# The gated one-hot of the last block: built with slots on the partitions from positions and scores spread through DRAM, instead of turned on TensorE

## The reference

```python
capacity = max(1, int(Sz * 2.0 / E) + 1)                       # 33 of 128 tokens
scores = softmax(einsum('bsd,ed->bse', x, router_w), axis=-1)  # E = 8
gate_vals, sel_idx = top_k(swapaxes(scores, 1, 2), capacity)   # for each sample and expert
tokens = x[b_idx, sel_idx]
h = gelu(einsum('becd,edh->bech', tokens, w1) + b1)
y = einsum('bech,ehd->becd', h, w2) + b2
out = zeros_like(x).at[b_idx, sel_idx].add(y * gate_vals[..., None])
```

## Time and profile before

| | us |
|---|---|
| three runs | 1085.27, 1085.51, 1091.91 |
| median | 1085.51 |
| span of the profiled execution, first to last instruction | 1077.5 |
| TensorE busy in it | 966.2 |
| DVE, ACT, POOL busy | 642.9, 571.7, 468.3 |

### The profile page before, as it was taken

One profiled execution on the slowest core, in us unless ns is written; L12 is line 12 of the kernel. 1 busy time (PEld: TensorE's weight loads), 2 busy tenths in 40 slices (PEclk: granted clock), 3 DMA queues, 4 the chain that ended last, 5 costly groups with the idle time before them and its releaser, 6 DMA issues. The chain is left out here.

```text
span 1077.5 us, 23011 instructions
## 1 busy us (share of the span) xinstructions
PE 966.2 (90%) x8722; PEld 747.5 (69%) x8726; DVE 642.9 (60%) x2007; ACT 571.7 (53%) x1209; POOL 468.3 (43%) x752
## 2 busy tenths in 40 slices
PE   4889998998999799988989999888888999999998
PEld 2556666565656566777877887766667777778787
DVE  3657777677778564665763333446888457466241
ACT  4768887777676465423334332123333845755553
POOL 6246675758686744665520000233445244213010
PEclk9989999999999899999999999989999999999999
DMA  7756443323332120000002331300000331521421
GB/s 179 188 137 163 114 122 80 85 72 105 84 99 70 41 84 7 15 12 6 6 26 67 108 108 54 111 20 15 20 21 11 92 100 25 94 80 40 138 65 53
DMA packets 72942, 78.56 MB, mean 73 GB/s; under 512 B 8469, under 2 KB 64132, under 8 KB 72832
## 3 DMA queue, kind: packets, MB, share of 16 engines
q1 hardware_dynamic: 67104, 69.61, 23.2%
q0 software_dynamic: 4096, 6.84, 3.0%
q10 hardware_dynamic: 1632, 0.64, 0.3%
HBM read 38.25 MB, written 11.68 MB: 46 GB/s over the span
## 5 line engine op out<-in xcount | busy, mean ns | idle before, releaser
L1286 DVE TENSOR_REDUCE arena<-pb 128x8 f32<-128x1024 f32 (+1 forms) x128 | 128.4, 1007 | 60.0 <-PE pb L647 56.5
L1780 ACT ACTIVATE arena<-pb 128x1024 f32<-128x1024 f32 (+1 forms) x128 | 130.8, 1022 | 58.9 <-PE pb L663 51.0
L2292 POOL DMA_INDIRECT arena<-yd,arena x64 | 63.9, 999 | 141.4 <-issue 141.3
L1834 ACT ACTIVATE arena<-pb 128x256 f32<-128x256 f32 x128 | 48.0, 383 | 131.0 <-PE pb L832 103.6
L831 PE MATMUL pb<-XLT,arena 128*128 128x256 f32 x256 | 80.2, 396 | 10.0 <-DVE arena L1445 7.5
L680 PE MATMUL pb<-arena 77*32 77x128 f32 (+1 forms) x2048 | 85.1, 285 | 0.0
L2171 POOL DMA_INDIRECT xd<-XB,arena x64 | 64.0, 1000 | 33.1 <-issue 19.2
L832 PE MATMUL pb<-XLT,arena 128*128 128x256 f32 x256 | 78.0, 387 | 0.0
L2030 ACT ACTIVATE arena<-pb,arena 128x264 f32<-128x264 f32 x128 | 54.7, 482 | 37.4 <-PE pb L1135 37.3
L2088 POOL TENSOR_SCALAR arena<-arena 128x4 f32<-128x4 f32 x48 | 9.4, 196 | 147.2 <-DVE arena L1241 144.8
L1441 DVE SCALAR_TENSOR_TENSOR arena<-arena,pb 128x256 f32<-128x256 f32 x128 | 53.0, 414 | 25.5 <-ACT arena L1834 19.7
(11 more groups left out here) (233 smaller groups left out, 2386.1 us busy)
## 6 DMA issues: line engine op xcount, KB each, us to landing
arena<-arena SPq DMA_DIRECT2D x190, 128.0 KB, 2.4
arena<-in_pe SPq DMA_DIRECT2D x32, 514.5 KB, 3.7
arena<-in_pr SPq DMA_DIRECT2D x8, 768.0 KB, 5.0
arena<-arena SPq DMA_DIRECT2D x43, 77.0 KB, 2.2
xd<-arena SPq DMA_DIRECT2D x8, 320.0 KB, 3.0
arena<-xd SPq DMA_DIRECT2D x8, 320.0 KB, 5.7
yd<-arena SPq DMA_DIRECT2D x8, 320.0 KB, 5.2
XO<-in_x SPq DMA_DIRECT2D x8, 256.0 KB, 3.2
```

The source lines that it names most:

```text
L1286: e.tensor_reduce(NM[i % 2][0][:, b, 4 * h:4 * h + 4, :].rearrange("p t h -> p h t"), sc, AX, ALU.max, negate=True).then_inc(v_max, 1)
L1780: e.activation(PT[n % 2][0:nk, :], bk2[1][0:nk, :], ACT.Exp, scale=SC8).then_inc(a_exp, 1)
L2292: e.indirect_dma_start(G[x % 8], None, yd, bass.IndirectOffsetOnAxis(ap=IDG.bitcast(U32)[:, k, b:b + 1], axis=0), bounds_check=None, oob_i ...
```

## The change

OTP is written with slots on the partitions at once. Slots are cut in three groups of 11 per expert (SLW = 11), so that a group has 8 x 11 = 88 partitions (RT). SP writes CS and TK of a unit to DRAM (`keep_places`), and at step 9 reads them back (`spread_places`), expert by expert, broadcast over the 11 partitions of the expert, to REP (88 x 8 samples x 2 x 128). At steps 33 to 40 DVE computes `ot`: for each of the three groups the position row is compared with the slot number of the partition (a new constant) and multiplied by the score row, in one instruction. OTP has three buffers now, so `ot` of a sample waits for `place` of the third sample before it. `og`, `gated` and `ot` on ScalarE are gone. `yt` writes YT in the order sample, group, expert, slot; `back` and `place` use three groups of 88 instead of 99, 99 and 66; `ys` is one activation instead of two.

```diff
@@ SP
+            def keep_places(u):
+                L.wait_ge(v_cs, u + 1)
+                L.wait_ge(v_tk, 2 * u + 1)
+                e.dma_start(pd[u, :, 0, :], CS[u % 2]).then_inc(d_pd, 16)
+                e.dma_start(pd[u, :, 1, :], TK[u % 2]).then_inc(d_pd, 16)
+
+            def spread_places(u):
+                L.wait_ge(d_pd, 32 * (u + 1))
+                if u:
+                    L.wait_ge(v_ot, 8 * u)
+                else:
+                    L.wait_ge(p_dn, 16)
+                for x in range(8):
+                    src = pd[u, :, :, :].rearrange("(b e) n t -> e b n t", e=8)[x].unsqueeze(0)
+                    e.dma_start(REP[SLW * x:SLW * x + SLW], src.to_broadcast([SLW, 8, 2, 128])).then_inc(d_rp, 16)
+
             for t in range(SLOT0, SLOTS + 1):
+                for g in group_at(t, 34, 1):
+                    keep_places(g // 2)
                 for u, k in esteps(t):
+                    if k == 9:
+                        spread_places(u)
                     if k in range(18, 34, 2):
@@ TensorE
-            def gated(u, b):
-                x = 8 * u + b
-                B = 2 + b % 2
-                og = OHP[b % 4][1].rearrange("p e s -> p (e s)")
-                L.wait_ge(g_og, x + 1)
-                L.wait_ge(*free[B])
-                for k, (a, n) in enumerate(TI):
-                    ins = e.transpose(bat(bk[B], k)[0:n, :], og[:, a:a + n], ident)
-                ins.then_inc(p_ot, 1)
-                free[B] = (a_ot, x + 1)
@@ place
-                L.wait_ge(a_ot, x + 1)
+                L.wait_ge(v_ot, x + 1)
@@ VectorE
+            def ot(u, b):
+                x = 8 * u + b
+                L.wait_ge(d_rp, 128 * (u + 1))
+                if x >= 3:
+                    L.wait_ge(p_bo, x - 2)
+                for k in range(3):
+                    ins = e.scalar_tensor_tensor(OTP[x % 3][:, k, :], REP[:, b, 0, :], CST[0:RT, C_SL + k:C_SL + k + 1],
+                                                 REP[:, b, 1, :], ALU.is_equal, ALU.mult)
+                ins.then_inc(v_ot, 1)
+
             def yt(u, k):
...
-                e.tensor_scalar(YT[:, :, k * CAP2:(k + 1) * CAP2], bk[4][:, 0:N8].rearrange("p (b s) -> p b s", b=8),
+                to = YT.rearrange("p b (k e s) -> p b k e s", k=3, e=8)[:, :, :, k, :]
+                e.tensor_scalar(to, bk[4][:, 0:N8].rearrange("p (b k s) -> p b k s", b=8, k=3),
                                 EWP[q % 4][:, 1028:1029], None, ALU.add).then_inc(v_yt, 1)
...
                         yt(u, (k - 16) // 2)
+                    if k in range(33, 41):
+                        ot(u, k - 33)
                     if k == 39:
                         put(2 * u)
@@ ScalarE: ot is removed, and ys becomes
-                e.activation(o[:, 0:2, :].rearrange("p k t -> p (k t)"), bk[B][0:99, 0:256], ACT.Copy)
-                e.activation(o[0:66, 2, :], bk[B][0:66, 256:384], ACT.Copy).then_inc(a_ys, 1)
+                e.activation(flat(YSP[x % 3]), bk[b % 3][0:RT, 0:384], ACT.Copy).then_inc(a_ys, 1)
@@ POOL
-            def og(u, b):
-                x = 8 * u + b
-                o, g_ = OHP[b % 4]
-                L.wait_ge(v_oh, x + 1)
-                if x >= 4:
-                    L.wait_ge(p_ot, x - 3)
-                e.tensor_tensor(g_, o, SCO[u][:, b, :].unsqueeze(2).to_broadcast([128, 8, CAP2]), ALU.mult) \
-                    .then_inc(g_og, 1)
```

More of the change, by code:

```diff
@@ L364, in program @@
         TK, WK, M8, CS = ([r(64, n) for _ in range(2)] for n in (128, 128, 8, 128))
-        OHP = [(r(128, 8, CAP2), r(128, 8, CAP2)) for _ in range(2)]
+        OHP = [r(128, 8, CAP2) for _ in range(4)]
         rl = Region(KEEP, SF0)
@@ L376, in program @@
         EWP.append(r(128, 1029))
-        OHP += [(r(128, 8, CAP2), r(128, 8, CAP2))]
         ro = Region(SET0[3], SH0)
-        OHP += [(r(128, 8, CAP2), ro(128, 8, CAP2))]
         OUTP = [Region(ZB0, SET0[0])(128, GB, 128), ro(128, GB, 128)]
-        YSP = [r(99, 3, 128)]
         r = Region(SH0, WORDS)
-        OTP = [r(99, 3, 128) for _ in range(9)]
+        REP = r(RT, 8, 2, 128)
+        OTP = [r(RT, 3, 128) for _ in range(3)]
         HEP = [r(128, 4, N8) for _ in range(2)]
-        YSP += [r(99, 3, 128) for _ in range(2)]
+        YSP = [ro(RT, 3, 128)] + [r(RT, 3, 128) for _ in range(2)]
         msk = nc.dram_tensor("msk", (16, 32 * C), BF).ap()
         xd = nc.dram_tensor("xd", (E1 * CAP1, 128), F).ap()
+        pd = nc.dram_tensor("pd", (4, 64, 2, 128), F).ap()
         yd = nc.dram_tensor("yd", (E1 * CAP1 + 128, 128), F).ap()
@@ L402, in program @@
             sem("p_" + n) for n in ("tf", "w1", "w2", "t2", "rt", "cum", "gu", "dn", "tx", "gx", "dx"))
-        p_vb, p_te, p_re, p_tk, p_ps, p_xe, p_ot, p_e1, p_e2, p_ys, p_bo = (
-            sem("p_" + n) for n in ("vb", "te", "re", "tk", "ps", "xe", "ot", "e1", "e2", "ys", "bo"))
+        p_vb, p_te, p_re, p_tk, p_ps, p_xe, p_e1, p_e2, p_ys, p_bo = (
+            sem("p_" + n) for n in ("vb", "te", "re", "tk", "ps", "xe", "e1", "e2", "ys", "bo"))
         v_mv, g_y, v_ap = sems("v_mv", 5), sems("g_y", 5), sems("v_ap", 5)
@@ L410, in program @@
             sem("v_" + n) for n in ("w2", "lg", "ex", "sel", "cum", "idx", "idg", "h", "sh", "hr", "ye", "cb", "bgh"))
-        v_le, v_sco, v_tk, v_cs, v_oh, v_xe, v_yt, v_out = (
-            sem("v_" + n) for n in ("le", "sco", "tk", "cs", "oh", "xe", "yt", "out"))
+        v_le, v_sco, v_tk, v_cs, v_oh, v_ot, v_xe, v_yt, v_out = (
+            sem("v_" + n) for n in ("le", "sco", "tk", "cs", "oh", "ot", "xe", "yt", "out"))
         a_xt, a_f, a_exp, a_os, a_ont, a_tf, a_ge, a_t2, a_ex, a_th, a_xg, a_si, a_ye = (
@@ L415, in program @@
                                     "ye"))
[L416 to L418 removed]
+        a_te, a_he, a_ys, a_mid, a_va = (sem("a_" + n) for n in ("te", "he", "ys", "mid", "va"))
+        g_vo, g_bo, g_rest, g_a1, g_fb, g_f1, g_rs, g_tu = (
+            sem("g_" + n) for n in ("vo", "bo", "rest", "a1", "fb", "f1", "rs", "tu"))
         x_pe, x_act, x_dve = sems("x_pe", 2), sems("x_act", 2), sems("x_dve", 2)
@@ L1113, in gather @@
                 L.wait_ge(*free[B])
[L1114 removed]
+                e.matmul(bk[B][:, 0:N8], XB[:, x, :], OHP[b % 4].rearrange("p e s -> p (e s)"), start=True,
                          stop=True).then_inc(p_xe, 1)
                 free[B] = (v_xe, x + 1)
[L1118 to L1127 removed]
             def e_up(u, k, half):
@@ L1153, in back @@
                 L.wait_ge(*free[B])
-                for k, (a, n) in enumerate(TI):
-                    ins = e.transpose(bat(bk[B], k)[0:n, :], YT[:, b, a:a + n], ident)
+                for k in range(3):
+                    ins = e.transpose(bat(bk[B], k)[0:RT, :], YT[:, b, RT * k:RT * k + RT], ident)
                 ins.then_inc(p_ys, 1)
@@ L1166, in place @@
                     free[B] = (v_out, x // GB + 1)
-                for k, (a, n) in enumerate(TI):
-                    ins = e.matmul(bat(bk[B], b % GB), OTP[x % 9][0:n, k, :], YSP[b % 3][0:n, k, :], start=(k == 0),
+                for k in range(3):
+                    ins = e.matmul(bat(bk[B], b % GB), OTP[x % 3][:, k, :], YSP[x % 3][:, k, :], start=(k == 0),
                                    stop=(k == 2))
@@ L2049, in act @@
                 for u, k in esteps(t):
-                    if k in range(5, 13):
-                        ot(u, k - 5)
                     if k in range(13, 29):
@@ L2317, in pool @@
                     ln_scale(LNX, g)
-                for u, k in esteps(t):
-                    if k in range(0, 8):
-                        og(u, k - 0)
                 for g in group_at(t, 16):
```

23 lines of the change are left out of this document (8 added, 15 removed).

## The result

| | before | after |
|---|---|---|
| median | 1085.39 (1083.41 to 1091.91, 4 runs) | 1103.88 (1102.48 to 1105.88, 4 runs) |
| span of the profiled execution | 1077.5 | 1102.8 |
| ratio of the times | | 1.0142, 95% interval 1.0096 to 1.0189 |

The change makes the kernel slower by 18.5 us by the medians. The forecast was 10.4 us slower, at 1095.9; the time lies 0.9 us above the top of the range. The same kernel in six more runs on another chip came to 1.0184 of the kernel before (1.0148 to 1.0219).

A forecast was written before the change was run, and what follows sets the result against it. TensorE was busiest, but VectorE's queue order at the unit turns was taken to decide: 3.4 + 3.4 + 5.5 - 2.2 + 0.3 = +10.4 us on the 1085.51 median gave 1095.9 us; 8-in-10 range 1081 to 1103.

The forecast's parts named there:

- The work: Added VectorE instructions: three per `ot`, 0.286 us apart, 0.86 us per `ot`, 6.9 us per unit, 27.5 us in all.
- the DMA: Position and score writes and broadcasts on SP: broadcasts estimated at 5 to 8 us per unit, priced at nothing because covered.
- unit 0's stretch: Unit 0's own gathers, with no `ot` beside them, gain from less waiting and contention: -2.2 us.
- the end: Last transposes to the end of the kernel: eight `ot` and one `put` on VectorE, with small waits +0.3 us.
- the turn 0 to 1: From unit 0's experts to unit 1's: `ot` delays 5.7 us when gathers begin, part won back, given as +3.4 us.
- `r_cut`'s lateness: `ot` 0 to 4 ahead of `r_cut` on VectorE make it end 4.6, 4.6 and 2.8 us late in the three turns.
- What comes behind `r_cut`: `ot` 5 to 7 add 2.6 us per turn, less idle time and contention returned: -1.2, +0.9 and +0.6 us.
- the turn 1 to 2: From unit 1's experts to unit 2's: +6.5 us when gathers begin, 1.0 us won back, +5.5 us.
- 2 to 3: From unit 2's experts to unit 3's: 2.8 + 2.6 - 0.5 - 1.5 = +3.4 us.
- The clock rival: Pauses in the turns let TensorE's clock fall, about 1 to 2 us for each of three turns: 1098 to 1102; chance 0.15.
- TensorE's time is what counts: Rival: removing 10.6 us of TensorE transposes sets the time; full gain 1074.9, or 1078 to 1083; chance 0.19.
- The 8.0 us between span and median: Median above profiled span, placed ahead of first instruction, behind last, or in run spread; the sum was added to the median.

The follow-up runs named there:

- busy: Changed kernel plus small bf16 products on TensorE ahead of two of its waits (28 before `ps`, 24 before `place` 5); median 1099.1 us, 1.0101 of the kernel before.
- early8: Changed kernel with eight OTP buffers instead of three and all eight `ot` moved to steps 17 to 31, ahead of the turn; 0.9910 of the kernel before.
- again: The changed kernel, unaltered, in six more runs on another chip; 1.0184 of the kernel before.
- loadonly: Kernel before, gated transposes kept, plus 24 unread VectorE products per unit at steps 33 to 40 and their waits for `place`; 1.0210 of the kernel before.
- late8: Changed kernel with eight OTP buffers instead of three, `ot` left at steps 33 to 40; 1.0101 of the kernel before.
- early3: Changed kernel with only `ot` 0 to 2 moved, to steps 21, 25 and 29, three buffers kept; 1.0093 of the kernel before.
- third: Changed kernel with one of the three products per `ot` from the fourth sample on, output wrong; 1.0076 of the kernel before.
- latecut: Kernel before with five unread VectorE reductions directly ahead of `r_cut` of units 1, 2 and 3; 1.0134 of the kernel before.
- third8: Changed kernel with eight OTP buffers and one of three products per `ot` from the ninth sample on; 1.0028 of the kernel before.

## Why the forecast was right in direction and short in size

- **The work.** `ot` 0.86 us and 0.34 each (forecast 0.86 and 0.35), `oh` at a median of 0.42 us, `yt` unchanged at 0.49, the DMA hidden (6.3 us for the broadcasts, estimate 5 to 8), the expert phases unchanged, unit 0's stretch -2.2 (forecast -2.2), the end +0.1 (+0.3): right. Two of these were helped by luck. The 0.286 us from start to start came from a division by four where four starts have three intervals (0.254 by that row); measured are 0.26 to 0.28, so that an `ot` holds up the queue for 0.79 to 0.83 us, and 0.86 is its length. And of the eleven profiles without the gated transposes, six have unit 0's stretch at 19.8 us, but four at 23.9 and one at 23.2, with a lower clock in it.
- **The sum.** By its own terms the turn 0 to 1 was 5.7 - 0.4 - 0.95 - 0.75 = +3.6 and not +3.4; this changes nothing.
- **`r_cut`'s lateness.** Forecast 4.6, 4.6 and 2.8 us; measured by A 6.1, 4.5 and 2.4. In the turn 0 to 1 the clock was low from 889 to 893 already, where `place` 0 and 1 run, and `ot` 3 and 4 waited for them longer.
- **What comes behind `r_cut`.** The forecast had -1.2, +0.9 and +0.6 us there. Measured by B: -0.7, +6.7, +2.0. With less time at the low clock ("busy") B is 19.9 in the turn 1 to 2, +1.8. So the order of the queues was right, and the step that failed is the size of terms, one above all, because the sum had nothing for the clock: the turn 1 to 2 was forecast at +5.5 and was +11.1, of which about 5 us are the clock's (4.9 in "busy"). The turns 0 to 1 and 2 to 3 were 2.0 and 1.0 us more than forecast, +5.4 and +4.4 against +3.4 each.
- **The clock.** I had it as a rival with 1 to 2 us a turn and a chance of 0.15; it should have been part of the forecast. The prediction itself put a pause of about 3 us ahead of `ps` into each turn (5.2, 2.5 and 2.5 us were measured), and a pause of half that length, 1.48 us, already has a fall behind it in the earlier trace rows. The price was wrong as well: I took a fall as short as that one. In the turns of the kernel after, the clock was low for 10.2, 20.5 and 6.8 us. The clock rival's 1098 to 1102 was nearer to the result than the forecast, and still short. The Trainium skill's page TensorE: Matmul & The Clock Gate, in the section on HAM oscillation, has the clock fall when the engine idles, so that its next burst starts cold; the trace agrees in all three turns.
- **TensorE's time is what counts** fell: 10.6 us of TensorE's work were taken away and its busy time rose, 974.4 us against 966.2, because its products took longer at the low clock. The Trainium skill's page Perfetto Trace Analysis, in Identifying the Most-Contended Engine, says of the engine with the highest occupancy "Optimize this engine first"; here that paid only when VectorE's replacement work was kept out of the turn: early8 is that case.
- **The 8.0 us between span and median** were mostly spread, not overhead: in the four runs of the kernel after the span is 1.9 to 2.0 us below the time. It did no harm, since the sum was added to the median.

What stays open is why the low clock lasts. In the turn 1 to 2, after, again, loadonly and late8 have a pause of 1.53 us ahead of their pauses of 2.5 to 2.9, and the clock is low for 20.5, 20.5, 13.7 and 17.1 us in one piece. early3, third and latecut have 0.86 us there, as the kernel before has, and pauses of 1.65 to 2.98 behind it, and the clock is low for 6.8, 6.8 and 3.4 us; third8 has 0.86 and one of 2.04 and no fall. busy has the 1.53, shorter pauses behind it (0.94 and 2.05), and 3.4 us. So the long stretches go with the earlier pause of 1.53 us, which `ot` 0 and 1 bring about; whether it is their cause is not shown, since no run here varied the length of one pause and nothing else, and each kernel's turns were profiled once (the changed kernel's and early8's twice).

## What to carry to other kernels

Moving work off the busiest engine did not pay here while the work that replaced it landed in the queue of the engine that the busiest one was about to wait for. Look for the instruction behind which the next phase waits (`r_cut` here), put nothing ahead of it that could be done earlier, and give such work the buffers that it needs to be early; with eight buffers instead of three and another place in the order the same change is, on two chips, 0.5 and 0.9% faster than the kernel before instead of 1.4% slower. Where a forecast puts new pauses on TensorE as long as those that have a fall behind them in the trace (1.48 us in the earlier trace rows), put the clock's fall into the sum, and with the longest fall that can be read, not the shortest.

## What the hardware showed that was not expected

- Around pauses of 1.53, 2.49 and 2.91 us the granted clock fell to 0.50 and stayed there for 20.5 us, 17 of them with TensorE busy almost without a gap, and the next profile of the same kernel showed it again. In its other turns the same kernel came back to 1.00 after 3.4 or 6.8 us.
- In unit 0's stretch the same work ran at a mean clock of 0.71 in one execution and of 1.00 in another of the same kernel, 23.9 against 19.8 us.
- 3.02 us of VectorE work ahead of `r_cut`, three times, cost 12.1 us (latecut: 3.7, 4.1 and 4.3): about 1 us a turn came on top of the lateness, with 3.4 us more at the low clock.
